# A one-core decoder layer on Trainium2: expert weight ranges from squares on ScalarE, centring on GpSimd, scale vectors in PSUM, and a new order of the first turns

## The reference

```python
def bitlinear(x, w):                      # weights to -1, 0, 1; activations to 8 bits, one scale per row
    return einsum('bsd,ed->bse', act_quant(rmsnorm(x)), weight_quant(w))
# self-attention: for every row the 16 heads attend to each other, not the rows
scores = einsum('bshd,bstd->bsht', q, k) / Dh ** 0.5
ctx = einsum('bsht,bstd->bshd', softmax(scores), v)
ctx = swapaxes(ctx, 1, 2).reshape(B, S, D)
x = layernorm(x + bitlinear(ctx, wo))
x = layernorm(x + cross_attention(q=x, k=ctx_1024, v=ctx_1024))   # 16 heads over 128 rows
logits = x @ Wr.T + br                                            # 8 experts, the best 2 per row
h = relu(einsum('bsd,efd->bsef', x, W1) + b1)
o = einsum('bsef,edf->bsed', h, W2) + b2
x = layernorm(layer_norm(x + sum(o * router_w)) * gamma + beta)
```

## Time and profile before

| | us |
|---|---|
| median of 3 runs | 695.88 (688.09 to 696.74) |
| the profiled execution's own time | 695.81 |
| its span, first to last instruction | 694.1 |
| busy in the span: PE, DVE, ACT, POOL | 544.2, 539.0, 454.1, 478.4 |

### The profile page before, as it was taken

One profiled execution on the slowest core, in us unless ns is written; L12 is line 12 of the kernel. 1 busy time (PEld: TensorE's weight loads), 2 busy tenths in 40 slices (PEclk: granted clock), 3 DMA queues, 4 the chain that ended last, 5 costly groups with the idle time before them and its releaser, 6 DMA issues.

```text
span 694.1 us, 19937 instructions
## 1 busy us (share of the span) xinstructions
PE 544.2 (78%) x6596; PEld 446.3 (64%) x6596; DVE 539.0 (78%) x1603; ACT 454.1 (65%) x975; POOL 478.4 (69%) x658
## 2 busy tenths in 40 slices
PE   1488899899999946988887988887789999998200
PEld 0177787778779934766665766665568888986200
DVE  4889899999997567666979688897778666687584
ACT  4657689888984565667776776876545455667425
POOL 5357678777877365555778797996567776667653
PEclk9789999999999977799999899999699999999655
DMA  6802222222222534344420101001222333631231
GB/s 172 238 10 24 21 24 24 23 23 23 23 23 35 175 138 153 138 187 173 181 74 20 42 20 37 26 19 36 71 78 83 109 102 93 181 93 48 84 113 60
DMA packets 113108, 55.43 MB, mean 80 GB/s; under 512 B 70624, under 2 KB 103840, under 8 KB 113024
## 3 DMA queue, kind: packets, MB, share of 16 engines
q1 hardware_dynamic: 103984, 25.46, 16.3%
q10 hardware_dynamic: 4496, 19.02, 7.0%
q0 software_dynamic: 4544, 9.84, 4.1%
HBM read 21.25 MB, written 33.05 MB: 78 GB/s over the span
## 4 chain that ended last, share of the span: by engine, by line
PE 38%; DVE 19%; issue 13%; ACT 13%; POOL 9%; DMA 5%; SPq 1%; DVEq 0%; ACTq 0%; POOLq 0%
PE PS L1010 11%; DVE PS L1937 3%; POOL ys L899 3%; ACT W_raw L1580 2%; PE PS L1121 2%; PE PS L1132 2%; ACT prod L1588 2%; PE PS L1220 2%; PE PS L1311 2%; DMA W_raw<-in_L_ffn_W_dram 2%; POOL xs L839 2%; PE PS L1328 2%; PE PS L1330 1%; PE PS L1313 1%; PE PS L1329 1%
## 5 line engine op out<-in xcount | busy, mean ns | idle before, releaser
L1010 PE MATMUL PS<-prod,ident 128*128 128x144 f32 x1024 | 138.2, 295 | 8.8 <-DVE hctx L1917 8.5
L1010 PEld LDWEIGHTS PS<-prod,ident 128*128 128x128 f32 x1024 | 132.4, 196 | 16.6 <-issue 9.4
L779 POOL TENSOR_TENSOR prod<-prod,v 128x2048 f32<-128x2048 f32 x32 | 117.5, 3671 | 33.3 <-ACT prod L1425 33.3
L2201 DVE TENSOR_REDUCE m<-PS 128x8 f32<-128x1024 f32 x64 | 77.8, 1215 | 30.0 <-PE PS L1132 30.0
L899 POOL DMA_INDIRECT ys<-W_raw,ids x78 | 76.6, 982 | 30.1 <-issue 17.4
L1132 PE MATMUL PS<-prod 49*128 49x128 bf16 x1024 | 66.1, 232 | 26.6 <-ACT W_raw L1580 11.6
L2310 DVE SCALAR_TENSOR_TENSOR W_raw<-PS,W_raw 128x512 f16<-128x512 f32 x78 | 52.3, 688 | 37.3 <-ACT W_raw L1645 37.2
L839 POOL DMA_INDIRECT xs<-Y,spot_u x64 | 64.0, 1000 | 22.7 <-issue 14.4
L1937 DVE TENSOR_REDUCE PS<-pair_sq 128x128 f32<-128x1024 f32 x64 | 75.0, 1218 | 0.0
L1580 ACT ACTIVATE W_raw<-PS 128x1024 f32<-128x1024 f32 x64 | 65.8, 1028 | 11.8 <-PE PS L1137 11.8
L1132 PEld LDWEIGHTS PS<-prod 49*128 49x128 bf16 x1024 | 41.6, 100 | 46.5 <-issue 17.4
(11 more groups left out here) (325 smaller groups left out, 1574.7 us busy)
## 6 DMA issues: line engine op xcount, KB each, us to landing
xs<-pad ACTq DMA_DIRECT2D x16, 1152.0 KB, 4.9
Y<-xs SPq DMA_DIRECT2D x39, 144.0 KB, 2.3
W_raw<-ys SPq DMA_DIRECT2D x16, 256.0 KB, 3.4
W_raw<-in_L_ffn_W_dram SPq DMA_DIRECT2D x1, 2048.0 KB
shuffle<-hctx SPq DMA_DIRECT2D x32, 64.0 KB, 3.0
Y<-shuffle SPq DMA_DIRECT2D x32, 64.0 KB, 1.8
cs<-in_ctx_dram SPq DMA_DIRECT2D x8, 256.0 KB, 3.0
out_dram<-W_raw SPq DMA_DIRECT2D x8, 256.0 KB, 2.3
```

What stands on the lines that cost most here:

```text
L779: pool.tensor_tensor(rows[:, :, 0:D].rearrange("p t (d h) -> p t d h", d=HD), a.broadcast_to((P, H, HD, H)), v.broadcast_to((P, H, HD, H)) ...
L1010: last = pe.matmul(PS[:, 6, 0:TC], ident[:], prod2[:, i % 2, TC * t:TC * (t + 1)], start=(t == 0), stop=(t == H - 1))
L2201: dve.tensor_reduce(half_heads(m2[:], a), banks(a).rearrange("p r (g t) -> p r g t", t=P), AX.X, ALU.max).then_inc(max_done, 1)
```

## The change

- `square_weights` (ACT, new): squares of 1368 columns with their sum, one instruction in slot 0 of each turn of the loop, in place of DVE's maxima; three over W1, three over W2. `sum_squares`, `largest_squares` and the new `weight_scales` take the scales from the square sums, in PSUM; PE's turn and the spreading matmul now stand ahead of the first `sum_keys` after the loop.
- `center_experts(0..3)` (POOL, new): takes the last column off a quarter of W1 (8 x 127 columns) each; `expert` now consists of transposes. `center_router` and the epsilon of `mean_squares` move to POOL.
- amax1, clip1, rec1 and inv1sq lie in PSUM bank 5, columns 288 to 415.
- `x_scales` of the second tile comes before the first `pair_scores`, `round_x(1)` one slot earlier.
- `largest_y` stands between the two halves of slot 0's pair sums, `y_scale` between those of slot 1; in other slots one reduction takes all 256 sums.
- On PE the turns of the small weights in slot (1, 0) stand ahead of `sum_keys`.

```diff
-        amax1 = sb("amax1", [P, B])
+        amax1 = PS[:, 5, 288:288 + B]
-        clip1 = sb("clip1", [P, B])
-        rec1 = sb("rec1", [P, B])
+        clip1, rec1, inv1sq = (PS[:, 5, 288 + n * B:288 + (n + 1) * B] for n in range(1, 4))
...
+            def center_experts(n):
+
+                c = slice(n * E * FC // 4, (n + 1) * E * FC // 4)
+                pool.wait_ge(w_last_ready, 1)
+                pool.tensor_tensor(W1_raw[:, c, 0:D - 1], W1_raw[:, c, 0:D - 1], bc(w_last[:, c], D - 1), ALU.subtract
+                                   ).then_inc(w1_centered, 1)
...
                     weigh(u, j)
+                if isinstance(u, int) and (u, j) == (0, 2):
+                    center_experts(2)
                 if isinstance(u, int) and (u, j) == (0, 3):
-                    invert_rms(3, 2 * TB, 4 * TB)
+                    center_router()
+                    invert_rms(4, 2 * TB, 4 * TB)
+                if isinstance(u, int) and (u, j) == (1, 0):
+                    center_experts(3)
                 if isinstance(u, int) and (u, j) == (1, 2):
-                    invert_rms(4, 4 * TB, B)
+                    invert_rms(7, 4 * TB, B)
...
+            center_experts(0)
+            center_experts(1)
             turns(pool, 2, a_slot, ch, A_POOL_STEPS)
...
-                    pe.matmul(PS[:, banks[0], n * P:(n + 1) * P], W1_raw[:, c, :], ident[:], start=True, stop=False)
-                    pe.matmul(PS[:, banks[0], n * P:(n + 1) * P], w_last[:, c:c + 1].broadcast_to((P, P)), minus_ident[:],
-                              start=False, stop=True)
+                    pe.transpose(PS[:, banks[0], n * P:(n + 1) * P], W1_raw[:, c, :], ident[:])
                     last = pe.transpose(PS[:, banks[1], n * P:(n + 1) * P], W2_raw[:, g, n * P:(n + 1) * P], ident[:])
...
-            pe.transpose(PS[0:2, 7, 0:P], w_top_abs[:], ident[:]).then_inc(w_top_turned, 1)
+            pe.transpose(PS[0:2, 7, 0:P], w_square_sum[:], ident[:]).then_inc(w_top_turned, 1)
+            pe.wait_ge(w_top_ready, 1)
+            pe.matmul(PS[:, 7, 0:2], w_square_top[:].broadcast_to((2, P)), ident[0:2, 0:2], start=True, stop=True
+                      ).then_inc(w_top_spread, 1)
             sum_keys(T, 0)
             turn_rows(0)
             expert(0)
-            pe.wait_ge(w_top_ready, 1)
-            pe.matmul(PS[:, 7, 0:2], ones[0:2, :], w_top_diag[:], start=True, stop=True).then_inc(w_top_spread, 1)
...
+                part = bass.ds((SQUARED - 4) // 2 * (u - 2 - n), SQUARED)
+                act.activation(squares_out, weights[n][:, part], ACT.Square, scale=2.0 ** -20,
+                               accum_out=w_squares[:, bass.ds(u - 2, 1)]).then_inc(w_squared, 1)
...
+                if j == 0 and not isinstance(u, int):
+                    square_weights(u, parity)
+                if isinstance(u, int) and (u, j) == (0, 1):
+                    act.wait_ge(consts, 8)
+                    act.wait_ge(x_scaled, 2)
+                    round_x(1)
...
-                dve.tensor_tensor(W1_raw[:, :, D - 1], PS[:, 7, 0:E * FC], w_last[:], ALU.add).then_inc(w_ready, 1)
-                dve.wait_ge(w_ready, 1)
-                step(dve.tensor_reduce(w_top[:, 1:2], W1_raw[:, :, D - 1], AX.X, ALU.max, apply_absolute_value=True))
+                dve.tensor_copy(W1_raw[:, :, D - 1], PS[:, 7, 0:E * FC]).then_inc(w_ready, 1)
...
+                step(dve.tensor_scalar(top, top, 1e-36, None, ALU.max))
+                settle()
+                step(dve.tensor_scalar(top_bits, top_bits, 0xFE << 23, None, ALU.bitwise_and))
...
-            largest_weights()
+            sum_squares()
             context(T, 0)
+            largest_squares()
             pair_scores(T, 0)
-            join_largest()
+            weight_scales()
             context(T, 1)
-            weight_scales()
             largest_y(T - 2)
             low_weights(0)
```

More of the change, by code:

```diff
@@ L27, in decoder_layer @@
     ROUND = 1.5 * 2.0 ** 23
-    A_STEPS = 78
+    A_STEPS = 66
     A_POOL_STEPS = 16
@@ L695, in _, with invert_rms @@
                                pattern=[[-1, P]], channel_multiplier=1).then_inc(consts, 1)
+            def invert_rms(n, first, end):
+                b = slice(first, end)
+                pool.wait_ge(x_sq, n)
+                ch(pool.tensor_scalar(ssq1[:, b], ssq1[:, b], 1.0 / D, 1e-6, ALU.mult, ALU.add))
+                ch.settle()
+                pool.tensor_tensor(rms1[:, b], ssq1[:, b], half[:, b], ALU.pow).then_inc(x_rms, 1)
+            invert_rms(2, TB, 2 * TB)
             ch(pool.memset(pad[:], 0.0))
@@ L1042, in a_slot @@
                     turn_x(u + 1)
-                if there(-((j - 3) // TB)):
-                    sum_keys(u, j)
-                if j == 1 and there(2):
-                    turn_y(u - 2)
                 if isinstance(u, int) and u == 1 and j == 0:
@@ L1057, in a_slot @@
                     last.then_inc(small_psum, 1)
+                if there(-((j - 3) // TB)):
+                    sum_keys(u, j)
+                if j == 1 and there(2):
+                    turn_y(u - 2)
             turn_x(0)
@@ L1488, in a_slot @@
                     act.copy(W_T[:].rearrange("p a d -> p (a d)"), PS[:, 7, D:4 * D]).then_inc(small_ready, 1)
-                if j == 2 and there(0):
+                if j == 2 and there(0) and not (isinstance(u, int) and u == 0):
                     if isinstance(u, int):
-                        act.wait_ge(consts, 8)
                         act.wait_ge(x_scaled, u + 2)
@@ L1839, in spread_biases @@
+                last.then_inc(w_scaled, 1)
             def spread_biases():
                 dve.wait_ge(w_scaled, 1)
+                step(dve.tensor_scalar(b2_scale[:], w_scale[:, 0:1], w_scale[:, 1:2], X_SCALE, ALU.mult, ALU.mult))
+                settle()
                 step(dve.reciprocal(o_scale[:], b2_scale[:]))
@@ L1904, in norm_apply, with context @@
                 return last
-            def context(u, j, meanwhile=None):
+            def context(u, j):
                 k = TB * u + j
@@ L1928, in y_scale, with pair_scores @@
                 dve.reciprocal(s2[:], inv2[:]).then_inc(s2_ready, 1)
-            def pair_scores(u, j, scale_y=False):
+            def pair_scores(u, j, between=None):
                 k, i = TB * u + j, (j - 1) % TB
@@ L1935, in pair_scores @@
                 after(dve, pair_ready, 2 * k)
-                for first_sum, end_sum, total in ((0, D, sums[:, 0:D]), (D, 2 * D, sums[:, D:2 * D]), (2 * D, 2 * D + H, k2[:])):
-                    step(dve.tensor_reduce(total,
-                                           pair_sq[:, i % 2, HD * first_sum:HD * end_sum].rearrange("p (c d) -> p c d", d=HD),
+                joints = (0, D, 2 * D, 2 * D + H) if between else (0, 2 * D, 2 * D + H)
+                for first, end in zip(joints, joints[1:]):
+                    if between and first == D:
+                        between(u - 2)
+                    step(dve.tensor_reduce(k2[:] if first == 2 * D else sums[:, first:end],
+                                           pair_sq[:, i % 2, HD * first:HD * end].rearrange("p (c d) -> p c d", d=HD),
                                            AX.X, ALU.add))
-                if scale_y:
-                    y_scale(u - 2)
                 settle()
```

115 lines of the change are left out of this document (46 added, 69 removed).

## The result

The changed kernel takes 674.41 us (median of 4 runs, 672.81 to 676.38) against 693.87 before (688.09 to 696.74): a ratio of 0.972, with a 95% interval of 0.968 to 0.976. Forecast were 672.9 us, in a range of 665 to 687. The profiled execution took 676.38 with a span of 674.6; before it was 695.81 and 694.1. The forecast was worked out from that execution, so its gain of 22.9 us stands against 19.4 between the two profiled executions. That the forecast time lies only 1.5 from the median is partly luck, since the profiled execution of the changed kernel was the slowest of the four.

The account below looks back on a forecast made before the run. No engine alone bounds the kernel: PE and DVE, near full, wait for each other and for four-engine chains. Start 13.3, loop 4.2 and end of stage 5.4 make 22.9; 695.81 - 22.9 = 672.9 us, range 665 to 687.

Parts of the forecast that it names:

- Part A: First turns, to 70 us: W1's maximum and scale stalls leave DVE, work is reordered; 13.3 us off, bounds 4.9 to 15.2.
- The rival of half the start: Start: clock low in three more sums and a quarter slower, or PSUM not sparing stalls; 680 to 681.3; chance 0.13.
- Part B: The loop: DVE loses pieces of W2's maximum, Y's maximum comes earlier, ACT gets a Square; 4.2 us off.
- I take 0.75 a turn: Loop: saving per turn along ACT's chain from Y's landing to the turn of Y, Square included; 4.2 us in all.
- The prediction's own bound for a hidden Square: Loop: best case if the added Square on ACT were hidden, 1.3 us a turn, 8 in all.
- Part C: End of the first stage: cheaper turns of W1 and W2 on PE, earlier scales; 5.4 us off, bounds 1.0 to 10.6.
- the first rival: Experts' stretch: PE falls to its lower clock in transposes; about +3.2 us there instead of -5.4, time 681.5; chance 0.08.
- let the splits run at their own pace: End of the stage: behind the rounded Y, experts 3 to 7 go at 0.6 us on ACT, 0.7 on DVE each.
- The loop didn't give nothing: Rival: the loop gives nothing, with the Square at 2 us or Y landing later; 677.1 us; chance 0.10.
- The clock of the later stages: Slower rival, 250 to 640 us: granted clock falls from 0.92; 0.80 cancels the gain, 0.75 gives 706.4; chance 0.04.

Follow-up runs that it names:

- the last two versions: Changed kernel with k2 moved before hctx, POOL's scale of Y earlier and add_x later: 672.88 us; that plus the next tile's scale of Y brought forward: 668.71 us.

## Why the prediction was right, and where its steps were not

**Part A** came out as forecast step by step: 13.3 us, with the pair sums at 20.60, context (2, 0) at 58.50 and no stall. Two things in it were off, and that the end came out to 0.1 is partly luck. The first sum took 5.01, not 6.0, so context (1, 1) came 0.9 early; of that 0.6 was left at context (2, 0) and nothing at the end. And the share of the place in PSUM was priced too low where the rival needed it: the 3.4 + 1.65 that the trace of before showed were the stalls of an order in which most scales happened to fall between weighs. In the new order, with POOL's work closer together, the start ends 11.5 us later with the same instructions in SBUF. So the start's gain is PSUM's first (11.5 when it is put back), W1's maximum second (2.2 at most). Together these are more than the 13.3, so they can't simply be added up; and with the vectors in SBUF all the rest of the change, new order included, is worth 82.29 - 80.47 = 1.8 there. The new order of the first turns by itself wasn't tried. The rival of half the start, had PSUM not helped, would have ended at 687, not 680.

**Part B** was the step that failed: "I take 0.75 a turn" was worked out along ACT's chain from Y's landing, with the Square on it. Shown instead: PE still waits 0.33 for that chain, but has 1.0 us to spare at its next wait, so the Square costs nothing (shortened: 22.54), and DVE's order of add_x and context (u, 3) sets the turn (add_x 0.58 shorter: turn 0.58 shorter). The prediction's own bound for a hidden Square, 1.3 a turn, fails by the same path: it is hidden, and the turn gained 0.34. The Square was longer than forecast too (1.49 from its start to the next instruction's; forecast 1.3), without effect. A piece of W2's maximum was worth 0.07 of the turn, not the 0.3 of its duration: it lay for the most part in a gap that stays when it goes. That two engines near full wait for each other was read rightly at the start; the chain followed for the sum then left DVE out.

**Part C**: sized 5.4, measured 3.8. Of the steps, the scales at 198.9 (5.2 us after the last sum, forecast 5.6) and ACT's first split at 201.4 (7.7, forecast 7.7) came as forecast. PE's wait for the rounded Y was 2.41, not 1.9. The step that failed is the one behind it, where the prediction let the splits run at their own pace; two things stood in their way. First, PE's clock fell for a short time, as windows of that stretch show:

```profile
210.90:213.50 2.60, 1.08 (x10) 0.84 (x8) 1.36 (x4) 1.71 (x5) 2.52 (x8) 1.00 0.65 207
213.50:216.90 3.40, 1.26 (x12) 1.05 (x12) 1.41 (x2) 3.37 (x7) 2.14 (x5) 1.00 0.31 40
216.90:220.40 3.50, 3.46 (x16) 3.14 (x17) 1.57 (x3) 1.45 (x3) 0.00 (x0) 0.51 0.42 142
220.40:223.30 2.90, 2.85 (x33) 2.57 (x31) 2.87 (x9) 0.00 (x0) 0.00 (x0) 1.00 0.97 377
```

PE was busy 2.34 of the 6.0 us before 216.90, and then a granted clock of 0.51, the lower level, holds until 220.4: expert 5's eight transposes go at 0.21 instead of 0.11, 0.8 us while ACT waits for them. In all ten traces with this wait of 2.4 us some transposes behind it take 0.21; in the four without it (before, the run in which TensorE takes the last column off, and the last two versions, where the wait is 0.80) none does. So a piece of the first rival was there, after holes, for 3.5 us. Elsewhere transposes of the experts ran at 0.11 and 1.00 (220.4 to 223.3 among them). The Trainium skill, TensorE: Matmul & The Clock Gate, section Part 4: PE-mode transpose, has it that transposes don't count as a busy PE for the clock in the same way. Matmuls stand between the transposes in all these stretches, so no run here tries that rule.

Second, the splits of experts 6 and 7 are queued on ACT behind casts that wait for DVE's qk_f, and DVE does add_x first. ACT's timelines, before and after:

```profile
243.81 0.51 ACT L1568 CAST pair_sq<-qk_f 128x384 bf16<-128x384 f32 x1 [4.34 <-DVE qk_f L2213]
...
224.55 0.51 ACT L1612 CAST pair_sq<-qk_f 128x384 bf16<-128x384 f32 x1 [4.34 <-DVE qk_f L2221]
```

From the start of DVE's split of expert 5 (239.50 before, 220.24 now) to the end of the last split it is 10.08 us in both, so no gain was to be had there. That add_x is on this path the run with the shorter add_x shows: 0.58 less of it, and 36.03 us from the loop's last sum to the last split instead of 36.63. The clock's 0.8 is half of the 1.6 that was missing; how the rest divides stays open.

**The other rivals.** The loop didn't give nothing, but half. The clock of the later stages stayed at 0.92, and the stretch behind the last split at 444 us.

## What to carry to other kernels

Before costing work added to one engine's chain, list for every wait of the loop how long ago its other conditions were met: a chain with 1.0 us to spare at its end took an added Square for nothing here, and a piece removed from a gap gave 0.07 us of its 0.3. A stall that depends on what another engine happens to run beside it must be re-priced in the new order, not taken from the old trace. When a wait is taken out, look at once what the same queue waits for next: here 3.7 of 4.8 us (by one trace each) went into the next wait, and came back when that one was removed too.

## What was unexpected in the hardware

- DVE's gap between the reciprocal and hctx is some 0.24 us in the loop (0.46 to 0.54 from start to start), and an instruction of 0.23 to 0.29 us fits into it almost free (0.48 with it); one of 0.35 makes it 0.56 to 0.62. Outside the loop the same pair goes at 0.28 to 0.30. What the loop adds there wasn't tried.
- POOL's subtraction of 1016 columns (1.88 us) holds DVE's SBUF instructions as its multiplication of 2048 does (3.67), and three of POOL's instructions in a row held three of DVE's, 8.1 us in all.
